# Moving one product of TensorE to the end of each slot in a decoder layer's attention

## The reference

```
x = x + attn(layernorm(x))            # rope, softmax over 512 keys
x = x + xattn(layernorm(x), ctx)      # causal self attention + attention over ctx, summed
x = x + moe(layernorm(x))             # softmax gate, argmax, 16 experts, capacity 256
attn:  softmax(q @ k.T / 4) @ v,  then @ W_out + b
```

## Time and profile before

| | us |
|---|---|
| median of 3 runs | 1837.69 |
| lowest, highest | 1825.07, 1842.83 |
| the profiled execution | 1832.97 |
| its span in the profile | 1831.2 |
| PE busy | 1441.5 |
| DVE busy | 1277.9 |
| ACT busy | 1040.1 |
| POOL busy | 495.4 |

### The profile page before, as it was taken

The page is one execution under the profiler, slowest core; times in us unless marked ns, Lnnn a source line. Parts: engine busy times, 40 slices in busy tenths (PEclk is TensorE's granted clock), DMA queues, the critical chain, the costliest instruction groups (busy, mean ns, idle before and its releaser), DMA issues.

```text
span 1831.2 us, 37114 instructions
## 1 busy us (share of the span) xinstructions
PE 1441.5 (79%) x14304; PEld 647.5 (35%) x14304; DVE 1277.9 (70%) x2610; ACT 1040.1 (57%) x2086; POOL 495.4 (27%) x350
## 2 busy tenths in 40 slices
PE   3368877887888888887887888878878868529998
PEld 1122222222223342423433323324234232128897
DVE  2376776777778777786776866857868748426775
ACT  1137666766767667565665655655646646605553
POOL 3344434434510010202203022012021120233554
PEclk9769899989989999998998978979989988759999
DMA  3712333443332233331332233323422331318772
GB/s 89 186 53 76 98 95 113 108 96 103 90 80 62 62 79 79 83 92 45 84 90 75 59 93 79 71 69 81 98 54 68 91 68 38 126 39 275 269 267 72
DMA packets 115636, 176.17 MB, mean 96 GB/s; under 512 B 25121, under 2 KB 85127, under 8 KB 109832
## 3 DMA queue, kind: packets, MB, share of 16 engines
q1 hardware_dynamic: 107536, 158.89, 32.7%
q0 software_dynamic: 5888, 14.24, 2.3%
q10 hardware_dynamic: 2048, 0.83, 0.2%
HBM read 102.72 MB, written 51.18 MB: 84 GB/s over the span
## 4 chain that ended last, share of the span: by engine, by line
PE 47%; DVE 24%; DMA 7%; issue 6%; POOL 5%; SPq 5%; ACT 3%; another core or an unknown queue 2%; ACTq 0%; POOLq 0%; DVEq 0%
DVE negmax L1004 15%; PE psO L603 11%; PE psM L396 9%; PE psS L626 7%; PE psK L396 5%; PE psK L656 4%; PE psS L396 4%; DMA shared<-shared 3%; DMA stack<-mrows 3%; ACT probs L852 2%; PE psM L685 2%; DVE parts L1065 2%; POOL shared L1251 1%; DVE stats L952 1%
## 5 line engine op out<-in xcount | busy, mean ns | idle before, releaser
L1004 DVE TENSOR_REDUCE negmax<-psS 128x1 f32<-128x512 f32 (+3 forms) x1536 | 869.8, 614 | 312.9 <-PE psS L626 156.3
L852 ACT ACTIVATE probs<-psK 128x512 f32<-128x512 f32 (+3 forms) x1536 | 752.7, 543 | 471.1 <-PE psK L656 263.5
L603 PE MATMUL psO<-probs,V 128*32 128x256 f32 (+1 forms) x5632 | 473.4, 411 | 24.8 <-ACT U L844 17.8
L626 PE MATMUL psS<-stack 48*128 48x512 f16 (+3 forms) x1536 | 296.6, 383 | 157.9 <-DVE negmax L1004 136.6
L656 PE MATMUL psK<-stack 50*128 50x512 f16 (+3 forms) x1536 | 295.2, 381 | 39.7 <-DMA stack<-mrows 31.1
L626 PEld LDWEIGHTS psS<-stack 48*128 48x128 f16 x1536 | 75.1, 94 | 501.8 <-DVE negmax L1004 378.6
L603 PEld LDWEIGHTS psO<-probs,V 128*32 128x32 f32 x5632 | 116.2, 112 | 220.6 <-issue 148.2
L1230 POOL TENSOR_TENSOR shared<-packed,recipB 128x1024 f32<-128x1024 f32 x8 | 18.9, 2357 | 366.8 <-DMA recipB<-recip_scratch 366.8
L1209 POOL TENSOR_TENSOR rstd<-lnt,minus_half 128x4 f32<-128x4 f32 x24 | 24.7, 1028 | 299.6 <-DVE lnt L968 299.5
L656 PEld LDWEIGHTS psK<-stack 50*128 50x128 f16 x1536 | 78.8, 98 | 63.6 <-DMA stack<-mrows 38.5
L396 PE MATMUL psM<-xT,wx 128*128 128x512 f16 x288 | 73.0, 391 | 13.5 <-DVE parts L1065 5.7
(11 more groups left out here) (153 smaller groups left out, 1857.8 us busy)
## 6 DMA issues: line engine op xcount, KB each, us to landing
spare<-in_L_ffn_w_dram SPq DMA_DIRECT2D x32, 1024.0 KB, 5.8
parts_scratch<-parts SPq DMA_DIRECT2D x192, 128.0 KB
stack<-parts_scratch SPq DMA_DIRECT2D x96, 256.0 KB, 7.0
stack<-parts_scratch SPq DMA_DIRECT2D x96, 128.0 KB, 4.4
packed<-U SPq DMA_DIRECT2D x192, 64.0 KB
recipB<-recip_scratch SPq DMA_DIRECT2D x48, 256.0 KB
shared<-shared SPq DMA_DIRECT2D x64, 128.0 KB, 2.5
probs<-back_scratch POOLq DMA_DIRECT2D x16, 258.0 KB, 3.1
```

The costliest lines, as they stand in the source:

```text
L603: mm = nc.tensor.matmul(psO[32 * i:32 * i + 32, q0:q1], v_of(par)[:, kt, 2 * g + i % 2 + PAIRS * (i // 2), :], probs[:, (unit + i % 2) % P ...
L626: mm = nc.tensor.matmul(psS[:, banks[hh], 0:n], stack_of(par, 0)[rows, hp, qt * P:(qt + 1) * P], stack_of(par, 1)[rows, hp, 0:n], start=Tr ...
L852: nc.scalar.activation(probs[:, t % P_RING, i, q0:T], psK[:, S_BANKS[t][i], q0:T], ACT.Exp, scale=SM_SCALE / (1 if b.kind == "A" else WSCA ...
L1004: nc.vector.tensor_reduce(negmax[:, g % 2, at:at + 1], psS[:, S_BANKS[u // 2][j], 0:n], AX_X, ALU.max, negate=True).then_inc(s["max_done"], 1)
```

## The change

In each slot PE issued AV, S, K, J. Now it issues AV, K, J, S. Nothing is added or removed, and no wait is changed: `maxima()` is called after the loop over the jobs in place of ahead of `exponents()`.

```diff
-                    maxima()
                     exponents()

                     for idx, (slot, name, j) in enumerate(jobs):
@@
                         mm.then_inc(s["jobs_done"], 1)

+                    maxima()
+
             pe.wait_ge(s["route_dve"], total["route_dve"])
```

## The result

The change makes the kernel slower by 8%: 1983.69 us (median of 4 runs, 1974.77 to 1987.18) against 1838.93 for the kernel before in the same session, a ratio of 1.0793 [1.0736, 1.085]. Forecast were 1900 us and at most 1948. The profiled execution took 1987.18 us, its span is 1985.4, the mean granted clock 0.871 (before 0.902).

The account below looks back on a forecast made before the run. The prediction saw a path alternating between PE and DVE, neither the bound alone. Terms of 26 + 29 + 4 + 6 = 65 us on 1832.97 gave 1898, forecast as 1900 us for the runs' median, range 1836 to 1948.

Parts of the forecast that it names:

- linked jobs: Jobs waiting for DVE's tail of the slot before: longer links cost 26 us in A bodies, 29 in B.
- the two V jobs of C: Slots 2 and 4 of C bodies: their eviction no longer covers DVE's wait for the next S, 0.65 us each.
- K's DMA: K waits 17 times for the group's maxima and now holds up S: 11 us at most, 6 taken.
- The step that failed: Jobs that wait for nothing run beside the reductions of the slot before instead of their own: cost 0.
- J8 to J10: Link in A bodies: a whole pair of reductions replaces one AV, 3.03 us becoming 3.69.
- J14 to J16: Link in B bodies: two pairs now stand before the eviction, 2.51 us becoming 3.47.
- J16 to J18: Link in B bodies: loses the pair of slot 16, 0.43 us.
- J22 to J24 of B: Link in B bodies: loses a full pair, with no AV in slot 23, 1.2 us.
- the gain behind J17: C bodies: J17 goes ahead of S17 during DVE's backlog; replay puts J22 0.65 us earlier.
- rival (c): The clock falls as well, one more slow stretch in each running body: 1948 us, chance 0.15.
- Rival (a): Phase shift only: longer links are paid by shorter PE waits before S, 1838 us, chance 0.13.
- Rival (b): K and jobs fill PE's waits before S at 154 places, saving 48 us: 1790 us, chance 0.12.

Follow-up runs that it names:

- after_again: The changed kernel timed once more, in the second session beside the kernel before: 1922.85 against 1777.32 us, 1.0811.
- e4: Changed kernel, but S first again in the 162 slots whose job waits for DVE's tail of the slot before: 1830.95 against 1777.8 us, 1.0322.
- e12: Changed kernel with the old order in linked slots 5 alone: 1961.0 against 1837.26 us, 1.0669.
- e16: e4 with the old order also in the slots of the v, out and negmax jobs: 1868.2 against 1833.97 us, 1.019.
- e17: e16 with the old order also in all slots without a job: 1831.95 against 1833.97 us, 0.9999.
- e9: Changed kernel with K issued three times in linked slots, same result: 1907.03 against 1777.32 us, 1.0724.
- e10: Kernel before, but in A bodies S goes out first, ahead of AV: 1768.37 against 1777.32 us, 0.9928.
- e7: Changed kernel, PE untouched, with DVE's evictions of v, out, negmax, proj, xT and ctxT ahead of the slot's reductions: 1797.58 against 1777.8 us, 1.0116.
- e6: Changed kernel, PE untouched, with DVE's evictions of v, out and negmax ahead of the slot's reductions: 1880.82 against 1777.8 us, 1.0599.
- e11: e10 with S last in slots 17, 19, 20 and 25 of C bodies: 1763.86 against 1777.32 us, 0.9923.

## Why the prediction was wrong, point by point

The sign was right, and so was the mechanism of the links; the size was not: 65 us were forecast and 145 measured. By parts:

| part | forecast | measured | from |
|---|---|---|---|
| linked jobs | 59 (A 26, B 29, C 4 net of its gain) | 92 | after_again less e4 |
| of these slot 5 | | 23 | e12 |
| unlinked jobs evicted in their own slot | 0 (the two V jobs of C are priced at 1.3 a body within the C term above) | 19, give or take 12 | e4 less e16 |
| slots without a job, K ahead of S | 6 (K's DMA) | 34 | e16 less e17 |
| all other jobs, 37 slots | 0 | 0 | e17 |

**The step that failed** is "For a job that waits for nothing, the change is close to a shift in phase, and I cost it at 0", and with it the view that a slot without a job only shifts. Each pair of reductions on DVE needs its S, and whatever stands ahead of S on PE hands its own waits on to DVE: the prediction saw that for K's wait for the DMA (6 us) but not for K's waits for ACT, nor for the 0.22 us of K behind each job. And a job's eviction in its own slot now stands behind a pair that comes late, as at J4. What was put at 0 to 6 us, the slots without a job (34) and the own-slot jobs (19), measured 53 us. e1, which only moves K ahead of S but does so in every slot, costs 30, which agrees with the 34. The second term that was mis-sized is the links, 59 us against 92.

**The single links were read right.** J8 to J10 3.65 us (forecast 3.69), J14 to J16 3.58 (3.47), J16 to J18 2.58 (2.30), J22 to J24 of B longer by 1.19 (1.2). The idle time right before J10 and J16 grew by less than the 0.6 to 1 us that was to be the sign, 0.52 (0.68 to 1.20) and 0.43 (0.63 to 1.06). The replay of a few rows by their own durations held to within 0.3 us each. The 1.23 us for a second pair stands in no row that is cited; the two pairs took 2.40 (491.38 to 493.78) against 1.23 + 1.20 = 2.43. And 1898 and 4.7 make 1903, not 1900, which changes nothing. The sum over the links was mis-sized all the same, 59 against 92. The `v` job of slot 4 was priced at 0.65 in C, where J4 to J5 grew by 1.39, and at nothing elsewhere. In C the forecast netted the gain behind J17 against the links; that segment did gain (0.95 us), while 29 to 5 lost 3.8 and 5 to 13 lost 2.9. How the remaining excess divides over links, and how much of it is the clock's, is not settled.

**The clock** stood in rival (c) with a chance of 0.15, as an event apart from the forecast case. It is no alternative to the longer waits: with the whole change the two come together. (In the slots without a job they don't: e16 is 34 us slower at the same mean clock as the kernel before beside it, 0.896 against 0.895 over all runs.) The time at the lower clock per body, worked out from the granted clock of the segments, rose from 11.4 to 15.4 us in A, from 13.1 to 22.8 in B and from 10.2 to 15.4 in C. In B much of that belongs to the chip of these two traces: on the chip of e9 it rose from 6.3 (e10, whose B bodies are as before) to 9.7. The argument against it, that each gap is only some 0.7 us longer, did not hold: a wait of 1.08 us stands in the stretch with 0.61 above. The Trainium skill, TensorE: Matmul & The Clock Gate, Part 1, tells of this form too, micro-idles between groups of matmuls as banks cycle that make the clock swing; the stretches at 1113 and 1117 and e9 agree with it. Its weight as a rival was too low, and the range, which added it to the forecast but to no larger case, ended at 1948 for that reason.

**Rival (a)** was partly there: PE's waits before S did shrink, by 58.6 us, while the jobs' waits for DVE grew by 80 (56.9 to 137.0). What it left out is DVE, whose waits for S grew by 206.8. As an account of the time it is ruled out. The rule of the Trainium skill, Perfetto Trace Analysis, section Identifying Performance Opportunities, by which repeated gaps can mean too few buffers, would, taken for this kernel, have put the change near 0. It doesn't fit these runs: with the same banks, order alone moved the time between 0.9923 and 1.1151. **Rival (b)** is false as a whole, and true in one place, slots 13 to 21 of C.

**The test that the prediction lacked** is the one of e7. Before the change PE had S ahead of the job and DVE the reductions ahead of the eviction. The change turned PE's order around and left DVE's. Turning DVE's as well gives back 125 of the 145 us with PE's order left as changed; on PE alone only e17 gives back more, and it undoes the change in 731 of 768 slots.

## What to carry to other kernels

Where two engines feed each other in turns, look whether they issue their pairs of work in the same order; before one program's order is changed, set the other's beside it and ask, for each of its instructions, what it will now stand behind. Put first in a slot what the other engine cannot do without, since anything ahead of it, even a product that costs 0.22 us, hands on its own waits. And do not price longer waits of TensorE apart from its clock: where waits lengthen all through a kernel, add the slower matmuls to the same case.

## What was not expected of the hardware

The kernel before takes 1834 to 1837 us on three of the five chips of these experiments, and 1777 on the other two. In the traces of the former DVE and ACT stop at about the same moments, and the trace names no instruction of this core as the cause (it writes `remote`). In the waits of the kernel before:

```profile
ACT probs L852 <- remote: 39.0, 11, 5.3
DVE negmax L1004 <- remote: 37.7, 13, 5.5
```

One such place, on DVE:

```profile
976.52 1.02 DVE L1004 TENSOR_REDUCE negmax<-psS 128x1 f32<-128x384 f32 x2 [4.40 <-remote]
```

All 25 such stops fall where POOL issues its indirect DMAs, one of them at 973.93:

```profile
973.93 0.97 POOL L1279 DMA_INDIRECT back_scratch<-shared,scatter_to  x1 [0.30 <-issue]
```

None of the eight traces from the two chips at 1777 us (e4 and e6 to e11, and the changed kernel of the second base) has such an entry, though POOL issues the same DMAs. Of a B body the segment 29 to 5 takes 17.96 us in the kernel before and 11.55 in e10. The change costs 145 us on either sort, so the ratios stand; what makes the difference between chips was not tried.
